# Second stage of a fused AdaLN + mixture-of-experts kernel: where the sums into the output, the row gathers and the reload of the hidden state are queued

## The reference, cut to what matters

```python
x = x + _L0_ffn_ref(_L0_cond_ref(x, cond_1024, W3, b3, W2, b2), gate_w, w_gate, w_up, w_down,
                    sw_gate, sw_up, sw_down)
# _L0_cond_ref: relu(((n * v + v.sum(1)) * relu(q @ W3 + b3)[:, None]) @ W2 + b2)     -> h
# _L0_ffn_ref(h): shared expert + routed experts
shared = (silu(h @ sw_gate) * (h @ sw_up)) @ sw_down
scores = softmax(h @ gate_w.T); topk_w, topk_i = top_k(scores, 6)
# each of 64 experts takes at most 64 tokens (rows of h):
y = (silu(buf @ w_gate) * (buf @ w_up)) @ w_down
out_slots = y[flat_i, slot] * topk_w          # summed over the 6 experts of a token
```

## Time and profile before

| What | Value |
|---|---|
| Time, median of 3 runs | 1211.64 us (1211.52 to 1211.75) |
| Profiled execution, its own time | 1211.44 us |
| Profiled execution, span of the core's instructions | 1209.6 us |
| PE busy | 1204.5 us (100%) |
| DVE, ACT, POOL busy | 857.4, 329.9, 272.9 us |
| Moved by DMA | 250.91 MB, mean 207 GB/s |

### The profile page before, as it was taken

The page is one execution under the profiler, slowest core; times in us unless marked ns, Lnnn a source line. Parts: engine busy times, 40 slices in busy tenths (PEclk is TensorE's granted clock), DMA queues, the critical chain, the costliest instruction groups (busy, mean ns, idle before and its releaser), DMA issues.

```text
span 1209.6 us, 15909 instructions
## 1 busy us (share of the span) xinstructions
PE 1204.5 (100%) x5705; PEld 889.3 (74%) x5705; DVE 857.4 (71%) x1868; ACT 329.9 (27%) x631; POOL 272.9 (23%) x246
## 2 busy tenths in 40 slices
PE   9999999999999999999999999999999999999998
PEld 8888888888888888888866666666666666666666
DVE  7998989988888898886656555664655664655652
ACT  4454243434324353343111111110111201111111
POOL 0000000000000000000136245263463553543421
PEclk9999999999999999999999999999999999999999
DMA  9946444372643626246767988989989889899863
GB/s 220 223 111 192 96 135 118 92 179 52 179 103 85 174 75 158 56 141 200 244 222 248 333 278 271 338 280 276 338 260 327 299 284 307 292 304 301 275 145 87
DMA packets 158999, 250.91 MB, mean 207 GB/s; under 512 B 22664, under 2 KB 93704, under 8 KB 157768
## 3 DMA queue, kind: packets, MB, share of 16 engines
q1 hardware_dynamic: 142528, 222.22, 58.3%
q0 software_dynamic: 14048, 25.18, 10.5%
q10 hardware_dynamic: 2344, 2.50, 0.7%
HBM read 197.14 MB, written 61.10 MB: 213 GB/s over the span
## 4 chain that ended last, share of the span: by engine, by line
PE 95%; DVE 3%; issue 0%; ACT 0%; DMA 0%; DVEq 0%; ACTq 0%
PE bank L1509 23%; PE bank L1510 22%; PE bank L1511 22%; PE bank L1713 13%; PE bank L1728 7%; PE bank L1535 2%; PE bank L1632 1%; PE bank L1631 1%; PE bank L1569 1%; PE bank L1567 1%; PE bank L1580 1%; PE bank L1638 0%; DVE x L951 0%; DVE xpart L955 0%; DVE x L968 0%
## 5 line engine op out<-in xcount | busy, mean ns | idle before, releaser
L1509 PE MATMUL bank<-hh,gu 128*128 128x512 f32 x704 | 278.0, 395 | 0.0
L1510 PE MATMUL bank<-hl,gu 128*128 128x512 f32 x704 | 274.2, 390 | 0.0
L1511 PE MATMUL bank<-hh,gu 128*128 128x512 f32 x704 | 274.1, 389 | 0.0
L629 POOL DMA_INDIRECT hg<-table,idx_quarter x128 | 126.5, 988 | 643.5 <-DVE idx_hi L1391 594.0
L1509 PEld LDWEIGHTS bank<-hh,gu 128*128 128x128 f32 x704 | 132.2, 188 | 39.1 <-issue 12.8
L1511 PEld LDWEIGHTS bank<-hh,gu 128*128 128x128 f32 x704 | 132.2, 188 | 27.8
L1510 PEld LDWEIGHTS bank<-hl,gu 128*128 128x128 f32 x704 | 132.2, 188 | 26.2
L697 ACT ACTIVATE ah<-prod 128x512 fp32r<-128x512 f32 x96 | 60.6, 632 | 302.6 <-DVE prod L1051 287.2
L1468 DVE STREAM_TRANSPOSE eactT<-eact 32x96 f32<-32x96 f32 (+1 forms) x512 | 133.9, 261 | 7.9
L1509 PE MATMUL bank<-sdh,ah 128*128 128x512 f32 x320 | 125.9, 393 | 0.0
L1510 PE MATMUL bank<-sdl,ah 128*128 128x512 f32 x320 | 124.6, 390 | 0.0
(11 more groups left out here) (132 smaller groups left out, 1672.8 us busy)
## 6 DMA issues: line engine op xcount, KB each, us to landing
wg<-in_L_ffn_w_gate_dram SPq DMA_DIRECT2D x64, 704.0 KB
wu<-in_L_ffn_w_up_dram SPq DMA_DIRECT2D x64, 704.0 KB
wd<-in_L_ffn_w_down_dram SPq DMA_DIRECT2D x64, 512.0 KB
table<-hrow SPq DMA_DIRECT2D x64, 256.0 KB, 4.3
x<-in_x_dram SPq DMA_DIRECT2D x60, 256.0 KB, 6.8
wd<-in_L_ffn_w_down_dram SPq DMA_DIRECT2D x64, 192.0 KB
out_dram<-outst SPq DMA_DIRECT2D x35, 256.0 KB
outst<-in_x_dram SPq DMA_DIRECT2D x32, 256.0 KB, 3.5
```

The costliest lines, as they stand in the source:

```text
L629: nc.gpsimd.indirect_dma_start(out=hg[p % 3][:, b, :], out_offset=None, in_=quarters, in_offset=bass.IndirectOffsetOnAxis(ap=idx_quarter[: ...
L1509: nc.tensor.matmul(o, st_h, mv_h, start=first_mm, stop=False)
L1510: nc.tensor.matmul(o, st_h, mv_l, start=False, stop=False)
L1511: return nc.tensor.matmul(o, st_l, mv_h, start=False, stop=last_mm)
```

## The change

It has three parts, all in the second stage. First, the two transfers of a chunk's `add_out` become two separate steps: `add_half` for j = 0 and 1 stands behind the scatters and gathers of the first unit after the chunk, `add_half` for j = 2 and 3 behind those of the second; each waits for the sum before it like any other, and `after_add[v]` is now the count after the second half. Second, POOL begins the scatters and gathers of unit n, for n below 32, only when the down weights that this unit loads (`down_in`) have landed. Third, SP issues the load of a chunk's hidden state one chunk earlier, behind `down` tile 2, except for chunk 9, whose load stays where it was.

```diff
         for kind, n, j in second_stage():
             if kind == "experts" and n > 0:
                 sums += 2
                 after_scatter[n - 1] = sums
+                if put_off:
+                    v, half = put_off.pop(0)
+                    sums += 1
+                    after_half[n] = v, half, sums
+                    after_add[v] = sums
             if kind == "down" and n < 2 * ND - 1 and j == J - 1:
-                sums += 2
-                after_add[n] = sums
+                put_off += [(n, 0), (n, 1)]
...
             for kind, n, j in second_stage():
-                if kind == "gate_up" and j == 1 and n + 1 < 2 * ND:
-                    load_hT(n + 1 - ND)
+                if kind == "gate_up" and n == ND and j == 1:
+                    load_hT(1)
+                if kind == "down" and j == 2 and n + 2 < 2 * ND:
+                    load_hT(n + 2 - ND)
...
-            def add_out(v):
+            def add_half(v, half, total):
                 pool.wait_ge(s.down_taken, J * v + J)
-                pool.wait_ge(s.added, 16 * (after_add[v] - 2))
-                for half in range(2):
-                    at = chunk_of(v) * CH + 2 * half * P
-                    nc.gpsimd.dma_start(of[at:at + 2 * P, :].rearrange("(j p) d -> p j d", p=P),
-                                        (outst2 if half else outst)[:, :, :],
-                                        accum_op=ALU.add).then_inc(s.added, 16)
+                pool.wait_ge(s.added, 16 * (total - 1))
+                at = chunk_of(v) * CH + 2 * half * P
+                nc.gpsimd.dma_start(of[at:at + 2 * P, :].rearrange("(j p) d -> p j d", p=P),
+                                    (outst2 if half else outst)[:, :, :],
+                                    accum_op=ALU.add).then_inc(s.added, 16)
...
                     ahead = n + 2 if n == 1 else n + 3
+                    if n < NP:
+                        for e in range(2):
+                            pool.wait_ge(down_in[e], 32 * (n + 1))
                     scatter(n - 1, 0)
...
-                if kind == "down" and n in after_add and j == J - 1:
-                    add_out(n)
+                    if n in after_half:
+                        add_half(*after_half[n])
```

More of the change, by code:

```diff
@@ L390, in second_stage @@
             assert p == NP + 1 and turned == NP
-        sums, after_scatter, after_add = 0, {}, {}
+        sums, after_scatter, after_add, after_half, put_off = 0, {}, {}, {}, []
         for kind, n, j in second_stage():
@@ L398, in adaln_moe_ffn_kernel @@
                 after_scatter[n - 1] = sums
+                if put_off:
[3 more added lines that the diff above has]
+                    after_add[v] = sums
             if kind == "down" and n < 2 * ND - 1 and j == J - 1:
-                sums += 2
-                after_add[n] = sums
+                put_off += [(n, 0), (n, 1)]
         SUMS = sums
+        assert not put_off
         HALVES = (slice(0, D // 2), slice(D // 2, D))
```

## The result

| What | Before | After |
|---|---|---|
| Time, median (the runs beside each other) | 1211.68 us | 1236.56 us (1230.95 to 1240.18, 6 runs) |
| Ratio, with its 95% interval | | 1.0205 (1.0181 to 1.0230) |
| Profiled execution, its own time (span) | 1211.44 us (1209.6) | 1239.33 us (1237.5) |

The change makes the kernel 2% slower, 24.9 us by the medians. The direction was forecast, the size was not: 1217.9 us stood in the prediction, and its range ended at 1229.0.

What follows compares the result with a forecast made beforehand. PE was taken to bound the kernel, filled throughout the second stage. Of 25.6 us for the halves 11.8 stay; less 2.1 reserve, 9.7; over 1.55, 6.3. 1211.44 + 6.3 = 1217.7, as median 1217.9 us; range 1211.4 to 1229.

Steps and rivals of the forecast that it cites:

- PE is full, and the order of sums is the thing that can become late: Second stage: PE fills every stretch; POOL's serial sums into the output work without rest for 516 us.
- Gate and early load cost nothing: Second stage: waiting for down weights and loading the hidden state earlier were costed at nothing; uncovered, 1.5 and 3.4 us.
- Where it shows: Signs: 14 steps of 7 to 11 us, DVE's copies waiting, PE gaps in late chunks, read-back 8 us later.
- The price of the halves: Order of sums: two steps of 6.85 us replace one of 10.04, 3.65 us more per chunk, 25.6 us for seven.
- my two ends of 11 and 52: Bounds on the halves' price: 11 us from POOL's issuing time, 52 us from a line through the loaded steps.
- The fixed part: Cost of a step in the order of sums besides its bytes: 3.65 us, read at the end without loads.
- my line: Step cost in the order of sums: 3.65 us plus 0.00624 us per KB, from an unloaded scatter and pair.
- What comes back: Order of sums: later scatters meet fewer loads; 54% of the price comes back, 46% stays, 11.8 us late.
- the repayment: While PE stands it asks for no weights, scatters take 4.45 instead of 6.9 us; each us stood is worth 1.55.
- the reserve: At the end, DVE's first add is done 2.1 us before `down` tile 3 needs the bank.
- Much slower: Rival: nothing comes back and DVE's standing delays a unit's transposes; 15 to 23 us, about 1229; chance 0.17.
- Not slower: Rival: the order recovers, its last landing moving by less than 2.1 us; time 1211.6; chance 0.25.

Runs made afterwards that it cites:

- The first three rows of the table: Adds one by one against together: at the kernel before's place (1234.24 us), behind the first unit (1238.15 us); third, the change against itself with sums together.
- the small steps alone: Kernel before with added 64 KB steps in the order of sums: one behind each chunk's pair, 1235.92 us; four behind chunk 10 only, 1225.06 us.
- the four small steps: Kernel before with four added 64 KB steps behind the adds of chunk 10 and none elsewhere: 1225.06 us, ratio 1.0099.
- the run with copies by halves: Changed kernel; DVE's copies of tiles 0 and 1 wait only for the previous chunk's first half, tiles 2 and 3 for the second: 1233.87 us.

## Why the prediction was right in direction and wrong in size

- **PE is full, and the order of sums is the thing that can become late.** Right. The chain has 11% of transfers, and the loss appears once as PE's stands with the lower clock behind them and once as the lateness of the last sum.
- **Gate and early load cost nothing.** Right by themselves and together (0.9997 to 1.0002). What they add beside the halves, some 0.5%, is not told apart.
- **Where it shows.** Mostly right: 14 steps, 6.7 to 14.1 us each where 7 to 11 was forecast, still released by the sum before; DVE's copies waiting for a sum; PE standing at d3 and at a unit's down product; a later read-back, though by 28.1 us and not by 8. The gathers queued behind a late sum, which the prediction names only under the gate, are the path in four of the other runs.
- **The price of the halves, 25.6 us.** Too small, but not by much: 30.6 to 34.1 us where only the wait differs, and inside my two ends of 11 and 52. "The fixed part is best read where nothing else moves" (3.65 us) was a wrong choice: beside loads a step of 64 KB, which my line puts at 3.65 + 64 × 0.00624 = 4.05 us, takes 7.0 us on the average. The last of the seven, while 206 GB/s were moved, takes 5.32, and the one at 1033.98, at 338 GB/s, 7.65. (The stretch from 680.98 to 1196.88 is 515.9 us, not 516.7; the mean scatter stays 6.9.)
- **"What comes back" and the repayment.** This is the step that failed. I kept 46% of the 25.6 us, took off the reserve, and divided by 1.55 because a standing PE asks for no weights. Together that leaves 6.3 + 2.1 = 8.4 us of lateness, 33% of the price. In the change the last sum lands 28.1 us late, with the halves alone 18.5. The first three rows of the table keep 75% (22.9 of 30.6), 76% (26.0 of 34.1) and 78% (26.2 of 33.7), with every relief from PE's stands already in it. Against the small steps alone it is 58% (28.5 of 49.2) and 63% (17.2 of 27.2, in the longest of its executions), still above 33%. PE was to stand 6.3 us; it stands 21.1 us and is busy 6.8 us longer. With my own price and 77%, the sum is 25.6 × 0.77 − 2.1 = 17.6 us, about 1229; with the measured price and my discounts it is (33.7 × 0.46 − 2.1)/1.55 = 8.6. So the discounts were the larger error. The 54% was the mean load of the whole stage, not a share that a shift changes; and 1.55 assumed that the scatters beside a stand get the unloaded step. One or two do, as the 4.75 us at 896.09; the relief is short, for around 1070 us the loads fall to 39 GB/s for 5 us and are back at 256 GB/s behind them.
- **Not in the sum at all:** the lower clock behind each stand. It makes PE busy for 6.8 us longer. At the end, where nothing covers it, that is 1.9 us in tile 3.
- **The rivals.** "Much slower" (15 to 23 us, 1229) was nearest and still short, as it started from 25.6 us. "Not slower" is refuted by its own sign: the last landing moves by 28.1 us and not by less than 2.1. An order can catch up with its rows, as after the four small steps, but by then PE has stood.

The Trainium skill ("DMA: Bandwidth & Descriptors", section "Anatomy of one DMA — SWDGE (gpsimd) path") has about 2.0 us for the fixed part, by which seven chunks are an estimated 14 us; no run here bears that out, 30.6 and 34.1 us were measured where only the wait differs. The Trainium skill ("DMA: Bandwidth & Descriptors", section "Latency and other measured facts") says that this part is mostly the latency of the memory and smaller where the memory is lightly loaded. The direction agrees with 5.32 us at 206 GB/s and 7.65 us at 338 GB/s, one step each.

Left open: why 64 KB takes as long beside loads as it does; and why one of four executions of the run with copies by halves takes 1228.15 us and another 1245.38. Nothing was tried on either. No version is faster than the kernel before: with PE filled, there is nothing for one to gain, and the versions with the sums sent together equal it.

## What to carry to other kernels

Two transfers that a serial order lets go out together are one step of it; splitting them adds a fixed part, so price that part from steps beside the load that the stage really has. Follow a late order to whatever waits for it: here the copies, the gathers queued behind it on POOL, and the read-back at the end. Where PE is full, what it stands for any of them is lost, even if the order itself catches up later, so discount a lateness only by what a run shows. Moving such a pair to a later place was free here, while putting its halves one behind the other cost 2%.

## What the runs showed of the hardware

Beside loads, a transfer of 64 KB that adds into memory costs 5.3 to 8.2 us from start to start in this order, about as much as a scatter of 128 KB (6.9 us on the average). And a stand of PE costs more than itself. With four small steps behind chunk 10, PE stands 8.8 us at one product, and the stretch during and the one after it read:

```profile
878.00:888.00 10.00, 1.21 (x6) 0.30 (x4) 1.61 (x2) 0.00 (x0) 7.12 (x7) 0.72 0.69 198
888.00:893.00 5.00, 5.00 (x20) 2.04 (x18) 3.55 (x7) 3.93 (x8) 3.34 (x4) 0.53 0.32 56
```

The granted clock is 0.53 in the 5 us after it: nearly all of that stretch at 1.2 GHz, with PE busy throughout.
